# A DLRM tower on one core: when the second quad's rows are gathered and turned, and where the last sum over d stands

## The chip, the cores and the metric

One NeuronCore of a Trainium2 chip runs the whole program. The metric is device time of one execution in microseconds (us), as the median of three runs. Engines are named as the profile names them: PE is TensorE, ACT is ScalarE, DVE is VectorE, POOL is GpSimd, SP is SyncE, which here only issues DMAs.

## The reference

```python
e = jnp.stack([tbl_0[ids[:, 0]], ..., tbl_38[ids[:, 38]]], axis=1)   # (512, 39, 16)
Xi = X0 = e
for W, b in Ws:                                                      # three layers, H = 128
    Wr = W.reshape(H, F0_, Fi)
    Xi = jnp.einsum('hjk,bjd,bkd->bhd', Wr, X0, Xi) + b[None, :, None]
    res.append(Xi.sum(axis=2))
z = jnp.concatenate(res, axis=1)                                     # (512, 384)
h = jnp.concatenate([z, dense_ctx], axis=1)
h = jnp.maximum(h @ W_top1 + b_top1, 0.0)
h = jnp.maximum(h @ W_top2 + b_top2, 0.0)
y = h @ W_top3
```

Everything is float32. B = 512 batch rows, F = 39 fields, D = 16.

## The kernel before

The batch is cut in 32 tiles of 8 rows (8 rows by 16 d are 128 columns); four tiles are a quad, and there are 8 quads. I write (ti, g) for group g of tile ti in a quad; T counts tiles from 0 to 31.

**Gathering a quad.** POOL fetches its rows with ten indirect DMAs, `gather(q, g)` (L495). They are then regrouped into `emb_room`: for the first two quads by copies on the engines (`regroup`, L347), later by DMAs of SP. POOL repeats them down `emb_room` (`repeat_rows`, L507 and L509, signal `emb_made`), PE turns them (`turn_rows`, L1059, signal `emb_turned`), and ACT copies the result to `x0` (`keep_x0`, L657, signal `x0_made`).

**Layer 0 of a quad.** When `x0_made` comes, SP issues 12 copies inside SBUF: four for `xa` (L367) and eight for the windows of `bz` (L390; two of them for chunk 1, six for chunks 2 to 5), then eight more for the last chunk. POOL multiplies chunk by chunk (`multiply(q, c)`, L526): chunk 0 waits for the four copies, chunk 1 for its two, chunk 2 for all six. PE sums the chunks into `ps_x1` (`layer0`, L1096), one chunk after a group of the tile that `SECOND_SUMMED_AFTER` names: chunk 0 after (1, 9), chunk 1 after (2, 1), chunk 2 after (2, 3), chunk 3 after (2, 5).

**Layer 1 of a tile.** PE makes ten groups (`layer1`, L1191 to L1193: three matmuls into one of five banks of `ps_y`, signal `y_made`). ACT scales seven of them into `prod` (L740), DVE the other three, groups 2, 5 and 8 (L962, L964). A group waits for the bank to be read by whoever had it five groups ago. DVE reduces `prod` in two steps: `reduce_early(T)` (L972), and `reduce_late(T)` (L980). In tiles 0, 3, 4 and 7 and from tile 8 on, POOL first adds two pairs (`add_groups(T, 0)` and `(T, 1)`, L531), and `reduce_early` waits for both. ACT scales group 0 of tile T + 1 only after `reduce_early(T)`. PE sums over d with `sum_d(T)` (L1215), ACT keeps it (`keep_g`, L749).

**What sets the order** is written by hand: each engine runs its own list strictly in order and waits on semaphores. For quad 1, POOL issues gathers 2 to 9 each behind a step of the head (the first quad's rows, x0, xa, products, sum); then `add_groups(0, 0)`, half of the regrouping, `repeat_rows(1)`, `add_groups(0, 1)`, the index of quad 2 and its first seven gathers, then `multiply(1, c)`. The other half of the regrouping is ACT's, after group 3 of tile 0. PE turns quad 1's rows after group 7 of tile 0, and ACT's `keep_x0(1)` follows at the same place.

**The end.** Layer 2 is folded into one matmul loop over the 39 fields (L1262 to L1264), whose weights come by DMA from DRAM; the known parts of the first dense layer (`known_mlp1`: L1203 for the dense features, L1209 for parts 0 and 1) are put in around it. The split of the dense features into high and low parts is ACT's (L782, L783) and DVE's (L1035, L1037) in tile 29.

Of the kernel before, what the change touches and what calls it, by code (L numbers as in the profile page):

```python
# [5 lines left out]
ALU = mybir.AluOpType  # L6
# [3 lines left out]
F32 = mybir.dt.float32  # L10
# [3 lines left out]
P = 128  # L14
# [5 lines left out]
TILES = B // TB  # L20
# [3 lines left out]
QUADS = TILES // QT  # L24
# [8 lines left out]
CHUNKS = STEP + 1  # L33
# [6 lines left out]
GATHERS = -(-F // FPG)  # L40
# [68 lines left out]
SECOND_REGROUPED_AFTER = 3  # L109
NEXT_TURNED_AFTER, NEXT_KEPT_AFTER = [(0, 7), (0, 1)], [(0, 7), (0, 3)]  # L110
# [68 lines left out]
def build(nc, dense_ctx, ids, bases, table, W_top1, b_top1, W_top2, b_top2, W_top3, W0, b0, W1, b1, W2, b2, out):  # L179
# [8 lines left out]
    with ExitStack() as ctx:  # L188
# [290 lines left out]
        def _(pool):  # L479
# [13 lines left out]
            def gather(q, g):  # L493
                n = gather_rows(g)
                pool.indirect_dma_start(  # L495
                    out=rows[0:n, q % 2, g, :], out_offset=None, in_=table,
                    in_offset=bass.IndirectOffsetOnAxis(ap=index[0:n, q % 2, g:g + 1], axis=0),
                ).then_inc(gathered[q % 2], 16)
# [47 lines left out]
            pool.wait_ge(regrouped_dve, 1)  # L546
            gather(1, 2)
            pool.wait_ge(emb_made, 1)
            gather(1, 3)
            pool.wait_ge(first_x0, 1)  # L550
            gather(1, 4)
            pool.wait_ge(first_xa, 1)
            gather(1, 5)
            pool.wait_ge(first_z, 2)
            gather(1, 6)
            pool.wait_ge(first_z, 4)
            gather(1, 7)
            pool.wait_ge(first_summed, 1)
            gather(1, 8)
            pool.wait_ge(first_x1_lo, 1)  # L560
            gather(1, 9)

            add_groups(0, 0)
            pool.wait_ge(pool_step, 1)
# [74 lines left out]
            for T in range(FREE_QUADS * QT, TILES):  # L639
                for part in range(2):  # L640
                    add_groups(T, part)
                    between(T // QT, T % QT, part)

        @block.scalar
        def _(act):
# [105 lines left out]
            for T in range(TILES):  # L751
# [3 lines left out]
                for g in ACT_GROUPS:  # L755
# [14 lines left out]
                    if (T, g) == (0, SECOND_REGROUPED_AFTER):  # L770
                        act.wait_ge(gathered[1], 16 * GATHERS)
                        for f in range(FPG // 2):
                            ins = regroup(nc.scalar.copy, 1, f)
                        ins.then_inc(regrouped_act, 1)
# [4 lines left out]
                    if (T, g) == (TILES - 3, 4):  # L779
                        act.wait_ge(late_mlp, 16 * 6)  # L780
                        act.wait_ge(z_used, CHUNKS * QUADS)
                        nc.scalar.copy(dense_stack[0:C, :], dense_t[:]).then_inc(dense_hi_made, 1)  # L782
                        nc.scalar.copy(dense_w_stack[0:C, :], wt1[0:C, K1 // P, :]).then_inc(dense_hi_made, 1)  # L783
# [28 lines left out]
        def _(dve):  # L812
# [174 lines left out]
            for T in range(TILES):  # L987
# [45 lines left out]
                if T == TILES - 3:  # L1033
                    dve.wait_ge(dense_hi_made, 2)
                    nc.vector.tensor_tensor(dense_low, dense_t[:], dense_stack[0:C, :].bitcast(F32),  # L1035
                                            ALU.subtract).then_inc(dense_lo_made, 1)
                    nc.vector.tensor_tensor(dense_w_low, wt1[0:C, K1 // P, :], dense_w_stack[0:C, :].bitcast(F32),  # L1037
                                            ALU.subtract).then_inc(dense_lo_made, 1)
# [14 lines left out]
        def _(pe):  # L1053
# [195 lines left out]
            pe.wait_ge(act_step, ACT_STEPS * (TILES - 1) + ACT_GROUPS.index(YBANKS + 1) + 1)  # L1249
            for m in range(2):  # L1250
                known_mlp1(m, (3, 0))
            sum_d(TILES - 1)
            for part in (3, 0):
                for m in range(2, MC1):
                    known_mlp1(m, (part,))
            pe.wait_ge(g_kept, TILES)
# [8 lines left out]
            for m in range(MC1):  # L1265
                known_mlp1(m, (1,))
# [50 lines left out]
```

## Time and profile before

| | us |
|---|---|
| median of 3 runs (range) | 677.99 (677.51 to 680.46) |
| the profiled execution, its own time | 682.74 |
| span of the profiled execution | 680.5 |
| busy: PE, ACT, DVE, POOL | 654.7, 572.2, 518.0, 460.1 |
| PE's granted clock over the span | 0.992 |

A timeline row gives the start, the busy time, the engine, the line, what is written and read, the count, and in brackets the idle time before it and what ended it. Times are from the start of the span. The profiled execution took 2.2 us outside its span, and 4.75 us more than the median.

### The profile page before, as it was taken

How to read it: one execution, taken by the hardware profiler on the slowest of the kernel's cores; microseconds unless marked ns; L12 is line 12 of the kernel's file. 1: busy time of each engine (PE TensorE's matmuls, PEld its weight loads, DVE VectorE, ACT ScalarE, POOL GpSimd, SP SyncE). 2: the span in 40 equal slices, each digit the busy share in tenths (PEclk: the TensorE clock that was granted, in tenths of full speed). 3: DMA queues.
4: the chain of work that ended last, by engine and by line, in shares of the span. 5: the costliest groups of instructions: out<-in, count | busy, mean ns of one | idle time of the engine just before them, and what ended most of it. 6: DMA issues, size and time to landing. Idle time of an engine off the chain costs nothing. (4 is left out here: it accounts for less than half of the span.)

```text
span 680.5 us, 10678 instructions
## 1 busy us (share of the span) xinstructions
PE 654.7 (96%) x2692; PEld 480.2 (71%) x2692; DVE 518.0 (76%) x1017; ACT 572.2 (84%) x2013; POOL 460.1 (68%) x453
## 2 busy tenths in 40 slices
PE   3699999999999999999999999999999999999998
PEld 3566776677777777777777677767777777776673
DVE  5458796787878879697878778777868787888880
ACT  2467897889898989899999889888988899899772
POOL 6468779877787878787887888777878656333000
PEclk9789999999999999999999999999999999999999
DMA  7203143323342516142331313131313221204400
GB/s 212 57 14 101 8 104 68 74 54 89 92 118 35 175 15 189 15 137 44 110 70 37 83 20 99 16 103 16 97 12 95 24 71 41 89 1 134 176 0 0
DMA packets 111121, 49.22 MB, mean 72 GB/s; under 512 B 82907, under 2 KB 94903, under 8 KB 111060
## 3 DMA queue, kind: packets, MB, share of 16 engines
q1 hardware_dynamic: 104830, 45.94, 25.6%
q0 software_dynamic: 5376, 1.45, 2.2%
q10 hardware_dynamic: 854, 1.16, 0.7%
q8 instruction: 21, 0.34, 0.2%
q14 instruction: 40, 0.33, 0.2%
HBM read 13.81 MB, written 5.24 MB: 28 GB/s over the span
## 5 line engine op out<-in xcount | busy, mean ns | idle before, releaser
L740 ACT ACTIVATE prod<-ps_y,xt 128x128 f32<-128x128 f32 x1792 | 492.8, 428 | 63.4 <-PE ps_y L1193 57.4
L1191 PE MATMUL ps_y<-w_hi,x_hi 128*128 128x512 f32 (+1 forms) x640 | 304.0, 475 | 7.6 <-DVE x_lo L928 3.3
L1193 PE MATMUL ps_y<-w_hi,x_lo 128*128 128x512 f32 (+1 forms) x640 | 249.2, 389 | 0.0
L1192 PE MATMUL ps_y<-w_lo,x_hi 128*128 128x512 f32 (+1 forms) x640 | 249.2, 389 | 0.0
L531 POOL TENSOR_TENSOR prod<-prod 128x512 f32<-128x512 f32 x120 | 155.1, 1292 | 90.7 <-ACT prod L740 85.6
L964 DVE SCALAR_TENSOR_TENSOR prod<-ps_y,xt,prod 128x128 f32<-128x128 f32 x576 | 163.5, 342 | 38.0 <-PE ps_y L1193 37.6
L495 POOL DMA_INDIRECT rows<-in_table,index x160 | 153.9, 962 | 47.0 <-issue 32.4
L1191 PEld LDWEIGHTS ps_y<-w_hi,x_hi 128*128 128x128 f32 x640 | 120.3, 188 | 63.7 <-issue 21.3
L972 DVE TENSOR_REDUCE prod<-prod 128x128 f32<-128x1536 f32 (+1 forms) x64 | 116.3, 1818 | 51.8 <-ACT prod L740 42.7
L1192 PEld LDWEIGHTS ps_y<-w_lo,x_hi 128*128 128x128 f32 x640 | 120.9, 189 | 43.4 <-issue 20.9
L1193 PEld LDWEIGHTS ps_y<-w_hi,x_lo 128*128 128x128 f32 x640 | 120.5, 188 | 26.0
L526 POOL TENSOR_TENSOR room<-room 128x512 f32<-128x512 f32 (+2 forms) x90 | 115.8, 1294 | 2.9 <-DMA room<-room 2.7
L980 DVE TENSOR_REDUCE x<-prod 128x128 f32<-128x1536 f32 x64 | 111.8, 1747 | 5.8 <-issue 2.5
L1096 PE MATMUL ps_x<-room,w0t 117*128 117x512 f32 (+5 forms) x186 | 95.9, 596 | 0.8 <-POOL room L526 0.7
L1215 PE MATMUL ps_g<-bd,x 128*128 128x320 f32 x128 | 45.5, 437 | 1.2 <-DVE x L980 1.1
L962 DVE TENSOR_SCALAR prod<-ps_y,xt 128x128 f32<-128x128 f32 x128 | 38.4, 341 | 3.9 <-PE ps_y L1193 3.9
L1096 PEld LDWEIGHTS ps_x<-room,w0t 117*128 117x128 f32 (+5 forms) x186 | 34.1, 189 | 9.0 <-POOL room L526 2.2
L749 ACT COPY g_all<-ps_g 128x320 f32<-128x320 f32 x64 | 31.4, 491 | 3.3 <-PE ps_g L1215 3.3
L1215 PEld LDWEIGHTS ps_g<-bd,x 128*128 128x128 f32 x128 | 22.9, 188 | 9.6 <-DVE x L980 5.1
L797 ACT CAST g_hi<-g_all 128x512 fp32r<-128x512 f32 x39 | 23.9, 621 | 3.3 <-PE ps_y L1264 0.4
L872 DVE TENSOR_TENSOR bd<-ps_tr,mask 128x1248 f32<-128x1248 f32 x16 | 23.1, 1444 | 0.0
L507 POOL COPY emb_room<-emb_room 128x312 f32<-128x312 f32 x15 | 6.6, 443 | 24.1 <-DMA emb_room<-rows 22.1
(149 smaller groups left out, 378.8 us busy)
## 6 DMA issues: line engine op xcount, KB each, us to landing
room<-room SPq DMA_DIRECT2D x75, 234.0 KB
room<-room SPq DMA_DIRECT2D x45, 78.0 KB
emb_room<-rows SPq DMA_DIRECT2D x168, 5.0 KB
rows<-in_table,index POOLq DMA_INDIRECT x160
w_hi_dram<-g_all SPq DMA_DIRECT2D x5, 512.0 KB
w_lo_dram<-g_all SPq DMA_DIRECT2D x5, 512.0 KB
g_all<-in_L_rec_W SPq DMA_DIRECT2D x9, 256.0 KB
g_all<-in_L_rec_W SPq DMA_DIRECT2D x4, 512.0 KB, 3.8
```

The costliest lines, as they stand in the source:

```text
L495: pool.indirect_dma_start(out=rows[0:n, q % 2, g, :], out_offset=None, in_=table, in_offset=bass.IndirectOffsetOnAxis(ap=index[0:n, q % 2, ...
L526: nc.gpsimd.tensor_tensor(bz[0:r, c, :], window, left if c == LAST else xa[0:r, :], ALU.mult).then_inc(z_made, 1)
L531: nc.gpsimd.tensor_tensor(prod[:, SLOT[a]:SLOT[a] + 2], prod[:, SLOT[a]:SLOT[a] + 2], prod[:, SLOT[b]:SLOT[b] + 2], ALU.add).then_inc(pool ...
L740: ins = nc.scalar.activation(prod[:, SLOT[k] + m // 2, :, m % 2], ps_y[:, g % YBANKS, m * H:(m + 1) * H], ACT.Copy, scale=xt[:, q % 2, ti, ...
L964: ins = nc.vector.scalar_tensor_tensor(out=a, in0=y, scalar=x, in1=a, op0=ALU.mult, op1=ALU.add)
L972: nc.vector.tensor_reduce(prod[:, BIASED, :, 0], prod[:, EARLY if adds(T) else EARLY_FIRST].rearrange("p n h l -> p h n l"), AX_XY, ALU.ad ...
L980: nc.vector.tensor_reduce(x2[:, T % 2, :], prod[:, LATE[T % 2]].rearrange("p n h l -> p h n l"), AX_XY, ALU.add).then_inc(reduced, 1)
L1096: nc.tensor.matmul(ps_x1[:], w, z, start=c == 0, stop=c == summed(q)[-1]).then_inc(z_used, 1)
L1191: nc.tensor.matmul(y, hi, w1_hi[:, cols], start=True, stop=False)
L1192: nc.tensor.matmul(y, hi, w1_lo[:, cols], start=False, stop=False)
L1193: nc.tensor.matmul(y, lo, w1_hi[:, cols], start=False, stop=True).then_inc(y_made, 1)
L1215: nc.tensor.matmul(ps_g[:, 0:(F + 1) * TB], x2[:, T % 2, :], bd[:, T // QT % 2, T % QT].rearrange("p j b -> p (j b)"), start=True, stop=Tr ...
```

## The change

The second quad's gathers 2, 3 and 4 now wait for `first_x0`, `first_z` and `first_x1_lo`; gathers 5, 6 and 7 wait for the 1st, 3rd and 5th group of layer 1; then comes `add_groups(0, 0)`, and gathers 8 and 9 wait for the 6th and 7th group. ACT's half of the regrouping moves from behind group 3 of tile 0 to behind group 9; PE's turn of the rows and ACT's `keep_x0(1)` move from behind (0, 7) to behind (1, 1). The split of the dense features goes from ACT and DVE in tile 29 to POOL in tiles 29 and 30. At the end, the third bank's known parts and one of the fourth's stand before `sum_d(31)`, and part 1 of banks 0 and 1 before the loop over the fields.

```diff
-SECOND_REGROUPED_AFTER = 3
-NEXT_TURNED_AFTER, NEXT_KEPT_AFTER = [(0, 7), (0, 1)], [(0, 7), (0, 3)]
+SECOND_REGROUPED_AFTER = (0, 9)
+NEXT_TURNED_AFTER, NEXT_KEPT_AFTER = [(1, 1), (0, 1)], [(1, 1), (0, 3)]
...
             gather(1, 1)
-            pool.wait_ge(regrouped_dve, 1)
+            pool.wait_ge(first_x0, 1)
             gather(1, 2)
-            pool.wait_ge(emb_made, 1)
+            pool.wait_ge(first_z, 2)
             gather(1, 3)
-            pool.wait_ge(first_x0, 1)
+            pool.wait_ge(first_x1_lo, 1)
             gather(1, 4)
-            pool.wait_ge(first_xa, 1)
-            gather(1, 5)
-            pool.wait_ge(first_z, 2)
-            gather(1, 6)
-            pool.wait_ge(first_z, 4)
-            gather(1, 7)
-            pool.wait_ge(first_summed, 1)
-            gather(1, 8)
-            pool.wait_ge(first_x1_lo, 1)
-            gather(1, 9)
+            for g in range(5, 8):
+                pool.wait_ge(y_made, 2 * g - 9)
+                gather(1, g)
 
             add_groups(0, 0)
+            for g in range(8, GATHERS):
+                pool.wait_ge(y_made, g - 2)
+                gather(1, g)
             pool.wait_ge(pool_step, 1)
...
+                if T == TILES - 3:
+                    pool.wait_ge(late_mlp, 16 * 6)
+                    pool.wait_ge(z_used, CHUNKS * QUADS)
+                    nc.gpsimd.tensor_copy(dense_stack[0:C, :], dense_t[:]).then_inc(dense_hi_made, 1)
+                    nc.gpsimd.tensor_copy(dense_w_stack[0:C, :], wt1[0:C, K1 // P, :]).then_inc(dense_hi_made, 1)
+                if T == TILES - 2:
+                    pool.wait_ge(dense_hi_made, 2)
+                    nc.gpsimd.tensor_tensor(dense_low, dense_t[:], dense_stack[0:C, :].bitcast(F32),
+                                            ALU.subtract).then_inc(dense_lo_made, 1)
+                    nc.gpsimd.tensor_tensor(dense_w_low, wt1[0:C, K1 // P, :], dense_w_stack[0:C, :].bitcast(F32),
+                                            ALU.subtract).then_inc(dense_lo_made, 1)
...
-                    if (T, g) == (0, SECOND_REGROUPED_AFTER):
+                    if (T, g) == SECOND_REGROUPED_AFTER:
...
-            for m in range(2):
-                known_mlp1(m, (3, 0))
-            sum_d(TILES - 1)
-            for part in (3, 0):
-                for m in range(2, MC1):
-                    known_mlp1(m, (part,))
-            pe.wait_ge(g_kept, TILES)
+            for m in range(MC1 - 1):
+                known_mlp1(m, (3, 0))
+            known_mlp1(MC1 - 1, (3,))
+            sum_d(TILES - 1)
+            known_mlp1(MC1 - 1, (0,))
+            pe.wait_ge(g_kept, TILES)
+
+            for m in range(2):
+                known_mlp1(m, (1,))
             for j in range(F):
...
-            for m in range(MC1):
+            for m in range(2, MC1):
                 known_mlp1(m, (1,))
```

The four instructions that POOL gains in tiles 29 and 30 are the ones that ACT and DVE lose there.

POOL before, from the second quad's gather 2 to the first copy of the regrouping; in brackets what a row waits for:

```order
L495 DMA rows<-in_table,index 128x16 [waits regrouped_dve]
L495 DMA rows<-in_table,index 128x16 [waits emb_made]
L495 DMA rows<-in_table,index 128x16 [waits first_x0]
L495 DMA rows<-in_table,index 128x16 [waits first_xa]
L495 DMA rows<-in_table,index 128x16 [waits first_z] x2
L495 DMA rows<-in_table,index 128x16 [waits first_summed]
L495 DMA rows<-in_table,index 96x16 [waits first_x1_lo]
L531 TENSOR_TENSOR prod<-prod 128x512 [waits act_step]
L347 COPY emb_room<-rows 32x10x4 [waits emb_turned,gathered_1,pool_step]
```

POOL now, the same stretch:

```order
L495 DMA rows<-in_table,index 128x16 [waits first_x0]
L495 DMA rows<-in_table,index 128x16 [waits first_z]
L495 DMA rows<-in_table,index 128x16 [waits first_x1_lo]
L495 DMA rows<-in_table,index 128x16 [waits y_made] x3
L531 TENSOR_TENSOR prod<-prod 128x512 [waits act_step]
L495 DMA rows<-in_table,index 128x16 [waits y_made]
L495 DMA rows<-in_table,index 96x16 [waits y_made]
L347 COPY emb_room<-rows 32x10x4 [waits emb_turned,gathered_1,pool_step]
```

Three gathers have moved behind groups of layer 1, and two more behind the first addition as well; what follows them on POOL is as before.

ACT before, from the copy of `xa`'s rest to the first groups of tile 1 (four `L740` rows are one group):

```order
L719 COPY room<-ps_g 128x384
L740 ACTIVATE prod<-ps_y,xt 128x128 x12
L347 COPY emb_room<-rows 32x10x4 x8
L740 ACTIVATE prod<-ps_y,xt 128x128 x12
L723 ACTIVATE x_hi<-ps_x,columns 128x384
L657 COPY room<-ps_tr 128x16x4x8
L740 ACTIVATE prod<-ps_y,xt 128x128 x24
```

ACT now (its lines have moved by 8):

```order
L727 COPY room<-ps_g 128x384
L748 ACTIVATE prod<-ps_y,xt 128x128 x24
L731 ACTIVATE x_hi<-ps_x,columns 128x384
L748 ACTIVATE prod<-ps_y,xt 128x128 x4
L347 COPY emb_room<-rows 32x10x4 x8
L748 ACTIVATE prod<-ps_y,xt 128x128 x8
L665 COPY room<-ps_tr 128x16x4x8
L748 ACTIVATE prod<-ps_y,xt 128x128 x12
```

The regrouping stands behind all seven groups of tile 0, and `keep_x0(1)` (L657, now L665) behind two groups of tile 1.

PE before, from the end of layer 1 to the loop over the fields:

```order
L1203 MATMUL ps_tr<-g_hi 128x512
L1209 MATMUL ps_tr<-r,emb_room 128x512
L1203 MATMUL ps_x<-g_hi 128x512
L1209 MATMUL ps_x<-r,emb_room 128x512
L1215 MATMUL ps_g<-bd,x 128x320
L1203 MATMUL ps_y<-g_hi 128x512 x2
L1209 MATMUL ps_y<-r,emb_room 128x512 x2
L1262 MATMUL ps_y<-g_hi,w_hi 128x512
```

PE now (its lines have moved by 1 to 3):

```order
L1206 MATMUL ps_x<-r,emb_room 128x512
L1200 MATMUL ps_y<-g_hi 128x512
L1206 MATMUL ps_y<-r,emb_room 128x512
L1200 MATMUL ps_y<-g_hi 128x512
L1212 MATMUL ps_g<-bd,x 128x320
L1206 MATMUL ps_y<-r,emb_room 128x512
L1206 MATMUL ps_tr<-g_all,emb_room 128x512
L1206 MATMUL ps_x<-g_all,emb_room 128x512
```

Three more matmuls stand ahead of the sum over d, and two from behind the loop now stand ahead of it.

## Rows read from the trace of the kernel before

**Rows 1.** The page: busy time, share and instructions of each engine.

```profile
PE 654.7 (96%) x2692; PEld 480.2 (71%) x2692; DVE 518.0 (76%) x1017; ACT 572.2 (84%) x2013; POOL 460.1 (68%) x453
```

**Rows 2.** Waits of PE: total us, times, longest us.

```profile
PE ps_y L1191 <- DVE x_lo L928: 3.3, 1, 3.3
PE ps_y L1191 <- DVE x_lo L879: 2.5, 3, 1.4
```

**Rows 3.** Timeline of POOL around tiles 0 to 2.

```profile
35.48 0.92 POOL L495 DMA_INDIRECT rows<-in_table,index  x1 [0.30 <-issue]
...
39.79 2.49 POOL L347 COPY emb_room<-rows 32x40 f32<-32x40 f32 x8
44.09 0.44 POOL L507 COPY emb_room<-emb_room 128x312 f32<-128x312 f32 x1 [1.82 <-ACT emb_room L347]
...
45.23 1.30 POOL L531 TENSOR_TENSOR prod<-prod 128x512 f32<-128x512 f32 x1 [0.53 <-ACT prod L740]
...
46.98 1.00 POOL L495 DMA_INDIRECT rows<-in_table,index  x1 [0.28 <-POOL index L489]
...
56.78 1.30 POOL L526 TENSOR_TENSOR room<-room 128x512 f32<-128x512 f32 x1
...
61.70 1.31 POOL L526 TENSOR_TENSOR room<-room 126x512 f32<-126x512 f32 x1
```

**Rows 4.** Timeline of ACT: before layer 1, and in tiles 0 and 1.

```profile
34.06 0.37 ACT L715 ACTIVATE x_hi<-ps_x,columns 128x128 fp32r<-128x128 f32 x1 [6.47 <-remote]
...
42.12 1.85 ACT L347 COPY emb_room<-rows 32x40 f32<-32x40 f32 x8
...
48.66 0.59 ACT L657 COPY room<-ps_tr 128x512 f32<-128x512 f32 x1
49.88 4.25 ACT L740 ACTIVATE prod<-ps_y,xt 128x128 f32<-128x128 f32 x16 [0.64 <-PE ps_y L1193]
```

**Rows 5.** Timeline of DVE: the early reduction of tile 0.

```profile
49.12 1.74 DVE L972 TENSOR_REDUCE prod<-prod 128x128 f32<-128x1536 f32 x1
```

**Rows 6.** Timeline of PE in tiles 0 to 2.

```profile
47.87 0.75 PE L1059 MATMUL ps_tr<-ident,emb_room 128*128 128x128 f32 x4
...
49.44 0.40 PE L1193 MATMUL ps_y<-w_hi,x_lo 128*128 128x512 f32 x1
...
58.23 1.10 PE L1096 MATMUL ps_x<-room,w0t 128*128 128x512 f32 x2 [0.44 <-POOL room L526]
...
63.07 1.12 PE L1096 MATMUL ps_x<-room,w0t 126*128 126x512 f32 x2
```

**Rows 7.** Timeline of SP's queue: the window copies of quad 1.

```profile
52.44 6.29 SPq L390 DMA_DIRECT2D room<-room  x8
```

**Rows 8.** DMA issues: count, KB each, median us to landing.

```profile
g_hi<-g_hi SPq DMA_DIRECT2D x4, 32.0 KB, 1.9
```

**Rows 9.** Windows: stretch, busy us of PE, PEld, DVE, ACT, POOL, PEclk, DMA share, GB/s.

```profile
34.00:36.00 2.00, 1.13 (x4) 0.97 (x5) 1.33 (x4) 0.93 (x3) 1.47 (x2) 0.91 0.21 63
36.00:38.00 2.00, 2.00 (x5) 0.58 (x4) 0.67 (x3) 1.92 (x8) 0.40 (x1) 0.50 0.09 12
38.00:40.00 2.00, 2.00 (x7) 1.18 (x6) 0.13 (x1) 0.37 (x2) 1.48 (x2) 0.74 0.02 4
```

**Rows 10.** Timelines of PE, ACT and DVE in tiles 29 to 31 and after.

```profile
609.82 0.60 ACT L782 CAST g_hi<-dense_t 16x512 fp32r<-16x512 f32 x1
...
614.44 0.67 DVE L1035 TENSOR_TENSOR g_hi<-dense_t,g_hi 16x512 fp32r<-16x512 f32 x1
...
614.58 0.50 PE L1191 MATMUL ps_y<-w_hi,x_hi 128*128 128x512 f32 x1 [0.33 <-DVE prod L964]
...
618.47 0.50 PE L1191 MATMUL ps_y<-w_hi,x_hi 128*128 128x512 f32 x1 [0.23 <-DVE prod L964]
...
632.05 0.81 PE L1215 MATMUL ps_g<-bd,x 128*128 128x320 f32 x2 [1.09 <-DVE x L980]
```

**Rows 11.** All gathers (L495): ns min/median/max, first and last start.

```profile
L495 POOL DMA_INDIRECT rows<-in_table,index x160: 918/946/1155, 3.6 to 526.7; - x160
```

More of the change, by code:

```diff
@@ L778, in _ @@
                         keep_x0(q + 2)
[L779 to L783, printed above, removed]
                     if g == 7 and T > 0:
@@ L1032, in _ @@
                                             w2_home(False, n), ALU.subtract).then_inc(w2_lo_made, 1)
[L1033 to L1038, printed above, removed]
                 if T == TILES - QT:
```

## The prediction

> **What bounds the kernel now.** I read the page's busy line first [rows 1]: PE is busy 96% of the span, and no other engine is over 84%. The second view is the list of PE's waits [rows 2]. Its longest once matmuls run is 3.3 us before the first group of layer 1; the waits for `x_lo` at the quads' borders come to 2.5 us in three. From there on PE simply works through its list. So two things matter: an idle time of PE that the change adds is not won back later, because 650 us of work stand in a row behind it; and a relief of ACT, DVE or POOL brings only what PE waits for them.
>
> The third view is the timelines around tiles 0 to 2. They show that quad 1's layer 0 comes just in time. PE's chunk 0 waits 0.44 us for POOL at 58.23 [rows 6]. POOL's product of chunk 2 runs from 61.70 to 63.01 [rows 3], and PE takes it at 63.07 [rows 6]. So whatever delays POOL's chunk 2 by more than nothing delays PE as much, and everything after it.
>
> **The move of gathers, regrouping, turn and x0.** I follow what chunk 2 hangs on. Before, ACT regroups at 42.12, in a time when it would wait for PE, POOL repeats the rows from 44.09 to 44.70 (the addition at 45.23 has 0.53 us of idle time ahead of it), the addition ends at 46.53, and `keep_x0(1)` ends at 48.66 + 0.59 = 49.25 [rows 3, 4]. Now the same steps stand in this line, each waiting for the one before:
> - Group 9 of tile 0 is ready on PE at 49.84 (49.44 + 0.40) [rows 6]. The turn no longer stands ahead of it, which is 0.5 us: 49.3.
> - ACT scales it: 16 scalings took 4.25 us, so four take 1.1 [rows 4]: 50.4.
> - ACT regroups, 1.85 us [rows 4]: 52.3. It waits for all gathers. Gather 9 follows the seventh group, now at about 46.2. Its landing time is no row; before, POOL's regrouping at 39.79 did not wait for the gather issued at 35.48 [rows 3], so it lands within 4.3 us, by 50.5, and I cost this wait at nothing.
> - POOL repeats the rows, 0.6 us, and only then makes `add_groups(0, 1)`, 1.30 us [rows 3]; with handoffs of 0.05 to 0.1: 54.35.
> - DVE's `reduce_early(0)` waits for that addition, 1.74 us [rows 5]: 56.2. Before, it started at 49.12, so it is some 5 us late.
> - ACT's group 0 of tile 1 waits for that reduction, then group 1: 2.1 to 2.2 us. Only behind them stands `keep_x0(1)`, 0.59 us: 59.05.
>
> So x0 is ready at 59.05 instead of 49.25, 9.8 us later. PE meanwhile stops at the turn from about 50.7 to 53.1 (for `emb_made`) and at (1, 3) from 54.35 to 57.0 (for DVE's group 8, which stands behind the reduction). These idle times lie inside the delay of chunk 2 and are not added to it.
>
> From x0 to chunk 2 there are two paths. **POOL's own list:** the addition ends at 54.35 instead of 46.53; seven gathers at 0.95 + 0.30 us follow the index (which starts them 0.45 us after the addition), up to 63.3; then chunk 0, a gather, chunk 1, a gather, 2.46 us a pair: chunk 2 could start at 68.2. Before, it was 61.70 [rows 3], so this path alone costs 6.5 us. **SP's copies:** before, the last window is issued at 52.44 + 6.29 = 58.73 [rows 7], 9.5 us after x0; now at 68.5. A landing takes 1.9 us for the nearest transfer with a figure, 32 KB inside SBUF [rows 8]: 70.4, the lower bound. The upper bound is that the windows landed just before 61.70, 12.45 us after x0: 71.5. So chunk 2 is 8.7 to 9.8 us late. The copies are large and landed while other copies ran, so I take a value in the middle, **+9.3 us**.
>
> **PE's clock.** With chunk 2 at 71.0, its product is there at 72.3; PE has done (2, 3) by about 69.15 and is idle for 3.2 us. The one idle time of that length in the trace is the 3.3 us before layer 1 [rows 2]. After it the granted clock is 0.91, 0.50 and 0.74 in three stretches of 2 us [rows 9], which is 0.18 + 1.0 + 0.52 = 1.7 us of lost clock; that is 3.4 us at 1.2 GHz in place of 2.4. I expect the same once after chunk 2: 1.7 us, of which a wait of 0.4 us for chunk 3 covers a part: **+1.3 us**, bounds 0 and 1.7. The idle times at 50 to 57 may also lower the clock, but PE's next work ends ahead of POOL's chunk 0 (64.7) either way, so that costs nothing.
> The Trainium skill (TensorE: Matmul & The Clock Gate, What's actually happening) says that the slow state is the default and that activity releases it. By it even the shorter stops could bring the slow clock; the fall in the windows' rows agrees that idleness does, and no row here shows a shorter one that did.
>
> **The dense split.** ACT loses 1.2 us (0.60 and its twin) and DVE 1.3 us (0.67 and its twin) in tile 29, where both delay the banks: PE waits 0.33 us at 614.58 and 0.23 us at 618.47 for DVE's group 8 [rows 10]. These go: **-0.55 us**. On POOL the casts and subtractions stand in its idle time. They come about a tile later than DVE's at 614.44 [rows 10], near 622; four small copies of SP at some 0.6 us and a landing of 1.9 us [rows 8] make 626.5. PE asks for them when layer 1 is done, which is two banks of known parts (about 3 us) and the wait of 1.09 ahead of the sum at 632.05: near 627.9. So I cost this at nothing, but over 1.4 us more of delay would be a wait. The weights of the last loop are issued behind them, up to 2.6 us later than now, and are first wanted about 3 us after that sum.
>
> **The last sum over d.** PE waits 1.09 us for DVE's last reduction, until 632.05 [rows 10]. Three more known matmuls (about 1.5 us) now stand ahead of it, so the wait is covered; the amount of PE's work is the same, so what is won is the idle time: **-1.1 us**. ACT's copy and the first high and low parts come about 0.3 us later, and PE has the two matmuls of part 1 to do in that time.
>
> **Sum.** 9.3 + 1.3 - 0.55 - 1.1 = +8.95 us. Against the profiled execution (682.74) that is 691.7; it stands 4.75 us above the median of 677.99. I put the difference on the median: **686.9 us**. Nothing in the head before layer 1 hangs on the gathers except POOL's own list, so I cost their removal there at nothing; bounds are in the second rival.
>
> **Rivals.**
> A. *POOL's list decides, not the windows.* If the copies land sooner, because fewer gathers run beside them, chunk 2 is 6.5 us late, and PE's idle time there is 0.4 us with no slow clock: 678.0 + 6.5 - 1.65 = 682.8 us. Against it: the issue of the copies alone takes 9.5 us after x0.
> B. *The head starts earlier.* ACT's first `x_hi` waits until 34.06 for something that the profile cannot name [rows 4], while the eight gathers run. If they cause it, layer 1 starts up to 3.3 us sooner and the 1.7 us of slow clock there go too: 686.9 - 5.0 = 681.9 us. Against it: PE's sum, for which ACT waits, shares nothing with POOL that a row shows.
> C. *Not slower.* The same mechanism as B, in the head, at its full price of 5.0 us and with the 1.65 us of the end. It decides once the chain behind x0 costs less than 6.65 us; its lower bound is the 6.5 us of POOL's list, without a slow clock: 677.99 + 6.5 - 6.65 = 677.8 us.
> D. *More is lost.* The clock falls before chunk 3 and after it, or the stacked dense features come late by 1 to 2 us: 690 us.
> E. *Gathers slow down beside DVE's work.* Every gather took 0.92 to 1.16 us, in the head and beside layer 1 alike [rows 11]. If each of the seven ahead of chunk 0 had to sit out one reduction of DVE, 1.74 us [rows 5], chunk 0 and all behind it would come 12 us later: 699 us.
> The Trainium skill (SBUF — State Buffer, A bandwidth-pool intuition that's wrong) says that such a DMA waits for its descriptors while DVE holds a shared port, about 620 ns against 3100 ns. The range of 160 gathers does not bear this out here.
>
> **How the numbers follow.** Chances: the forecast 0.66 (own range 685 to 689), A 0.13, B 0.08, C 0.04, D 0.07, E 0.01; 0.01 for a faster outcome that I have not named. The range goes from A to the lower part of D: 682.5 to 689.8. A measurement of this kernel tells 0.5% from no change, 3.4 us: faster means under 674.6, slower over 681.4. C is no change, with the low edge of A and B (0.04); slower is the rest.
>
> **What would show it.** In the profile after: ACT's regrouping near 50.5 and its `x0` copy near 58.5; DVE's first early reduction near 54.4; PE waiting for `emb_room` and for `prod` in tile 1, then two or three waits at L1096's place for POOL's `room`, the longest about 3 us, and a granted clock of 0.50 around 73 to 77; no wait at 614 and at the last sum over d. I am wrong if `x0` is copied before 55, if chunk 2 starts before 69, or if layer 1 starts before 34.

## The result, and the profile after

The changed kernel takes 685.08 us (median of 5; 682.98 to 686.73), the kernel before 678.05 (5 runs) beside it. The medians are 7.0 us apart. The ratio of the two kernels' runs is 1.0096, with a 95% interval of 1.0069 to 1.0123: **6.5 us slower** (4.7 to 8.3). The profiled execution took 686.73 us with a span of 684.2, so its span is 3.7 us longer than that of before, whose profiled execution (682.74) was 4.7 us above its kernel's median.

PE's list of waits in the changed kernel (total us, times, longest us), for [rows 2]:

```profile
PE ps_y L1188 <- DVE prod L967: 3.8, 7, 2.2
PE ps_tr L1056 <- DVE emb_room L911: 3.4, 1, 3.4
PE ps_x L1093 <- POOL room L526: 3.1, 3, 2.6
PE ps_tr L1056 <- POOL emb_room L509: 2.5, 2, 2.1
PE ps_y L1188 <- DVE x_lo L882: 1.3, 1, 1.3
```

From layer 1 on, three new waits of over 2 us stand there: for `prod`, for POOL's product `room`, and for the repeated rows `emb_room`. The 3.3 us before layer 1 are gone, but the head has a new stop of 3.4 us, at the turn of the first quad's rows (`emb_room L911`), where before waits 0.3 us.

The chain behind quad 1's rows, timelines of the changed kernel: ACT, then POOL, DVE, SP's queue (as in [rows 3 to 5, 7]):

```profile
32.59 0.37 ACT L723 ACTIVATE x_hi<-ps_x,columns 128x128 fp32r<-128x128 f32 x1 [4.63 <-PE ps_x L1156]
...
47.40 1.85 ACT L347 COPY emb_room<-rows 32x40 f32<-32x40 f32 x8
53.11 2.19 ACT L748 ACTIVATE prod<-ps_y,xt 128x128 f32<-128x128 f32 x8 [3.86 <-DVE prod L975]
55.12 0.64 ACT L665 COPY room<-ps_tr 128x512 f32<-128x512 f32 x1
```
```profile
49.38 0.44 POOL L507 COPY emb_room<-emb_room 128x312 f32<-128x312 f32 x1 [1.40 <-ACT emb_room L347]
...
49.95 1.27 POOL L531 TENSOR_TENSOR prod<-prod 128x512 f32<-128x512 f32 x1
...
60.49 1.31 POOL L526 TENSOR_TENSOR room<-room 128x512 f32<-128x512 f32 x1
...
68.12 1.26 POOL L526 TENSOR_TENSOR room<-room 126x512 f32<-126x512 f32 x1 [2.71 <-DMA room<-room]
```
```profile
51.32 1.75 DVE L975 TENSOR_REDUCE prod<-prod 128x128 f32<-128x1536 f32 x1 [5.11 <-POOL prod L531]
```
```profile
55.78 3.13 SPq L367 DMA_DIRECT2D room<-room  x4
58.95 6.29 SPq L390 DMA_DIRECT2D room<-room  x8
```

The rows form one chain. ACT regroups; POOL repeats the rows (it was idle for 1.40 us, waiting for ACT) and then adds; DVE reduces (idle for 5.11 us, waiting for POOL); ACT scales two groups (idle for 3.86 us, waiting for DVE). Only then comes `x0`, which ends at 55.76. POOL's chunk 2 starts 12.36 us after that and waits 2.71 us **for a DMA**, so the window copies decide and not POOL's own list.

PE in tiles 0 to 2 of the changed kernel, for [rows 6]:

```profile
50.03 0.75 PE L1056 MATMUL ps_tr<-ident,emb_room 128*128 128x128 f32 x4 [2.12 <-POOL emb_room L509]
...
53.91 0.80 PE L1188 MATMUL ps_y<-w_hi,x_hi 128*128 128x512 f32 x1 [2.20 <-DVE prod L967]
...
61.95 1.10 PE L1093 MATMUL ps_x<-room,w0t 128*128 128x512 f32 x2 [0.23 <-POOL room L526]
...
69.44 1.12 PE L1093 MATMUL ps_x<-room,w0t 126*128 126x512 f32 x2 [2.59 <-POOL room L526]
```

Chunk 2 is at 69.44 where it was at 63.07 [rows 6]: 6.37 us late. Windows of the changed kernel (columns as in [rows 9]); the granted clock is the third number from the right:

```profile
36.00:38.00 2.00, 2.00 (x9) 1.47 (x9) 1.14 (x5) 0.63 (x3) 0.94 (x1) 1.00 0.06 16
...
48.00:50.00 2.00, 0.00 (x0) 0.00 (x0) 0.00 (x0) 1.19 (x6) 0.62 (x3) 1.00 0.00 0
50.00:52.00 2.00, 1.67 (x7) 0.97 (x7) 0.68 (x1) 0.00 (x0) 1.72 (x3) 0.77 0.00 0
52.00:54.00 2.00, 0.10 (x1) 0.10 (x1) 2.00 (x5) 0.89 (x4) 1.61 (x2) 0.50 0.03 4
54.00:56.00 2.00, 2.00 (x5) 1.61 (x6) 2.00 (x2) 2.00 (x8) 1.47 (x2) 0.50 0.09 7
...
68.00:70.00 2.00, 0.56 (x2) 0.32 (x3) 0.19 (x1) 0.09 (x1) 1.73 (x2) 1.00 0.13 31
70.00:72.00 2.00, 2.00 (x9) 1.25 (x8) 0.00 (x0) 0.63 (x3) 1.98 (x3) 1.00 0.13 25
```

PE's clock stays whole at the start of layer 1, where before it was 0.50. It stands at 1.2 GHz from about 51.2 to 57.6 instead. PE had been idle for 2.12 us before 50.03 and had worked again for some 1.2 us when the clock fell; its second stop, of 2.20 us, came only after that. The clock does **not** fall after the 2.59 us ahead of chunk 2.

The end, PE's sums over d of tiles 28 to 31 (before: tile 31 at 632.05 after 1.09 us of waiting [rows 10]):

```profile
614.67 0.70 PE L1212 MATMUL ps_g<-bd,x 128*128 128x320 f32 x2
622.58 0.70 PE L1212 MATMUL ps_g<-bd,x 128*128 128x320 f32 x2
630.08 0.70 PE L1212 MATMUL ps_g<-bd,x 128*128 128x320 f32 x2
637.50 0.81 PE L1212 MATMUL ps_g<-bd,x 128*128 128x320 f32 x2
```

No wait stands ahead of the last one.

### The profile page after: what moved, and what is told of

Its sections match the earlier page's. It is cut to its first block and busy times, and to the rows that moved or that the text cites. A ratio compares the mean times of both kernels' runs of the same rounds, so it can differ in the third digit from the quotient of the medians.

```text
span 684.2 us, 10678 instructions
## 1 busy us (share of the span) xinstructions
PE 657.3 (96%) x2692; PEld 482.6 (71%) x2692; DVE 517.4 (76%) x1015; ACT 571.6 (84%) x2011; POOL 464.8 (68%) x457
## 5 line engine op out<-in xcount | busy, mean ns | idle before, releaser
L495 POOL DMA_INDIRECT rows<-in_table,index x160 | 155.0, 969 | 52.7 <-issue 31.8
```

What stands on the lines that cost most here:

```text
L495: pool.indirect_dma_start(out=rows[0:n, q % 2, g, :], out_offset=None, in_=table, in_offset=bass.IndirectOffsetOnAxis(ap=index[0:n, q % 2, ...
```

## The experiments

In the table, before_again to e_keep ran on one chip, which I call the faster one, and e_list, e_sem, e_all and e_best on another, the slower one. The kernel before takes 668.8 and 669.0 us on the first and 678.7 us on the second; in the first comparison it took 678.05. A ratio is always against the kernel before beside it, and the microseconds are that ratio times before's median. Differences of medians deviate from them by up to 0.8 us in most rows, by 1.1 in e_keep and by 2.1 in e_list. The changed kernel itself was not run beside the last four. To compare traces I cut each span in four pieces: the start of ACT's first `x_hi`; from there to PE's chunk 2 of quad 1; from there to the sum over d of tile 28; and from there to the first matmul of the last part of the dense layer (L1269 before). All are read from the timelines.

| kernel | ratio (interval) | us against before | x_hi | to chunk 2 | to sum 28 | to the end's matmul |
|---|---|---|---|---|---|---|
| before | | | 34.06 | 29.01 | 546.45 | 56.48 |
| changed | 1.0096 (1.0069 to 1.0123) | +6.5 | 32.59 | 36.85 | 545.23 | 55.06 |
| before_again | 1.0005 (0.9991 to 1.0019) | +0.3 | 26.39 | 27.35 | 543.97 | 56.00 |
| after_again | 1.0127 (1.0106 to 1.0148) | +8.5 | 26.87 | 36.78 | 543.37 | 54.58 |
| e_turn | 1.0142 (1.0120 to 1.0165) | +9.5 | 26.26 | 36.70 | 543.95 | 55.97 |
| e_both | 1.0161 (1.0130 to 1.0191) | +10.8 | 25.30 | 36.96 | 543.12 | 56.00 |
| e_gath | 1.0039 (1.0023 to 1.0055) | +2.6 | 25.82 | 29.50 | 543.43 | 55.99 |
| e_end | 0.9991 (0.9973 to 1.0009) | -0.6 | 27.65 | 27.36 | 542.72 | 55.04 |
| e_tail | 0.9983 (0.9971 to 0.9996) | -1.1 | 25.48 | 27.48 | 543.67 | 55.50 |
| e_keep | 1.0079 (1.0060 to 1.0097) | +5.3 | 27.55 | 34.43 | 543.08 | 54.57 |
| e_list | 1.0089 (1.0060 to 1.0118) | +6.0 | 31.38 | 33.29 | 552.25 | 54.56 |
| e_sem | 1.0008 (0.9983 to 1.0034) | +0.5 | 30.98 | 34.41 | 544.69 | 54.58 |
| e_all | 1.0062 (1.0039 to 1.0085) | +4.2 | 29.71 | 33.50 | 548.57 | 54.58 |
| e_best | 0.9947 (0.9926 to 0.9968) | -3.6 | 34.27 | 28.88 | 544.09 | 54.58 |

### The turn alone, and with the gathers

The question was whether the earlier head of the changed kernel (rival B) belongs to the gathers. e_turn:

```diff
-SECOND_REGROUPED_AFTER = 3
-NEXT_TURNED_AFTER, NEXT_KEPT_AFTER = [(0, 7), (0, 1)], [(0, 7), (0, 3)]
+SECOND_REGROUPED_AFTER = (0, 9)
+NEXT_TURNED_AFTER, NEXT_KEPT_AFTER = [(1, 1), (0, 1)], [(1, 1), (0, 3)]
```

> The kernel before with ACT's regrouping behind (0, 9) and PE's turn and keep_x0(1) behind (1, 1); the gathers and the end are those of before. Theory G (the earlier head of the changed kernel comes from the gathers that left it): the head is that of before, the first x_hi of layer 1 starts near 34.0, PE runs at half clock at 36 to 38, x0 of quad 1 ends near 59, chunk 2 on PE starts near 72.5 instead of 63.07, and the time is about 9 us over before, 687 us. Theory V (the two profiled heads differed by chance, the gathers do nothing to them): the time is that of the changed kernel plus its 1.65 us at the end, 686.7 us, and the head's place in the trace may be either. Both theories give nearly one time here; it is the kernel with both moves that tells them apart.

e_both has in addition the change's edit of the gathers:

> The kernel before with the gathers moved and the regrouping, the turn and keep_x0(1) moved, that is the changed kernel without anything of its end. Theory G: the head is as in the changed kernel (first x_hi near 32.6, no half clock at 34 to 40), chunk 2 on PE near 69.4, and the time is 2.5 to 3.5 us under that of the kernel with the turn moved alone: 683.5 to 684.5 us if that is 687, and the end is then worth little. Theory V: the same time as the kernel with the turn alone, 686.7 us, and the end's edits are worth the 1.65 us that I gave them.

Measured: +9.5 us (8.0 to 11.0) and +10.8 us (8.7 to 12.8). The gathers gave nothing back here: on this chip theory V holds and rival B doesn't. Its head had no long wait to give back, as before_again shows below. The turn alone has the whole loss. POOL's chunk 2 in e_turn, then in e_both:

```profile
61.64 1.27 POOL L526 TENSOR_TENSOR room<-room 126x512 f32<-126x512 f32 x1 [1.57 <-DMA room<-room]
```
```profile
60.94 1.26 POOL L526 TENSOR_TENSOR room<-room 126x512 f32<-126x512 f32 x1 [2.84 <-DMA room<-room]
```

`x0` ends at 49.42 and 48.48 there, so chunk 2 starts 12.2 and 12.5 us after it, and in both it waits for the copies. On PE chunk 2 stands 36.70 and 36.96 us after the first `x_hi`, where before_again has 27.35 (below): **+9.4 and +9.6 us**.

### The gathers alone

```diff
+            pool.wait_ge(first_x0, 1)
             gather(1, 2)
+            pool.wait_ge(first_z, 2)
             gather(1, 3)
             pool.wait_ge(first_x1_lo, 1)
-            gather(1, 9)
+            for g in range(4, GATHERS):
+                gather(1, g)
```

> The kernel before with only the gathers moved: gathers 2, 3 and 4 behind first_x0, first_z and first_x1_lo as in the changed kernel, 5 to 9 straight behind 4; regrouping and turn stand where they were. Gather 9 is issued near 40.5 (33.4 + six times 1.2), lands by 44, so ACT's regrouping at 42.1 may wait some 2 us, and the turn with it. Theory G: layer 1 starts 1.5 us earlier and without half clock, which gives back up to 3.3 us; with some 1 us lost at the turn the time is 675 to 676.5 us. Theory V: no gain from the head, 678 to 680 us.

Measured +2.6 us (1.5 to 3.7), outside of what theory G expects (1.5 to 3 us faster) while theory V's 0 to +2 overlaps with the interval. ACT's regrouping in this kernel:

```profile
35.47 1.86 ACT L347 COPY emb_room<-rows 32x40 f32<-32x40 f32 x8 [2.98 <-DMA rows<-in_table,index]
```

It waits 2.98 us for the gathers, and chunk 2 is 2.15 us late (29.50 against 27.35). So even this small delay of quad 1's rows is paid in full, and nothing comes back in the head.

### Before and the changed kernel once more

> The kernel before, unchanged, for a second trace of it beside the runs of this call. Theory V (the head's delays of some microseconds belong to single executions, not to the gathers): PE's sum of the head comes 8 us after ACT's first regrouping, as with the turn moved alone, ACT names PE for its wait and not something remote, there is no half clock at the start of layer 1, and chunk 2 on PE starts 27.3 us after the first x_hi. Theory G (eight gathers in the head delay it): the long wait and the half clock of the first trace are there again, and the distance is 29.0 us. The time is that of the kernel before, ratio 1.000.

> The changed kernel, unchanged, beside the parts. Sum of the parts as measured: turn and gathers +10.3 us, the end -0.1 us by its median or -0.9 us by its trace: 9.4 to 10.2 us over before (ratio 1.0141 to 1.0152). If the 7.0 us of its first comparison hold here too (1.0105), the parts don't add up and something in the whole gives 3 us back. Chunk 2 on PE 36.9 us after the first x_hi, as in its first trace.

ACT's first `x_hi` in before_again:

```profile
26.39 0.37 ACT L715 ACTIVATE x_hi<-ps_x,columns 128x128 fp32r<-128x128 f32 x1 [3.16 <-PE ps_x L1159]
```

PE's chunk 2 in the same trace:

```profile
53.74 1.13 PE L1096 MATMUL ps_x<-room,w0t 126*128 126x512 f32 x2
```

The wait of 6.47 us for something remote in [rows 4] is 3.16 us for PE here, with the same gathers; there is no half clock after it. Chunk 2 follows 27.35 us after it. The first trace of before has 29.01, and the difference of 1.7 us is what [rows 9] lose to the clock. The changed kernel costs 8.5 us (7.1 to 9.9) on this chip, which overlaps with its first comparison; the 9.4 to 10.2 that I expected lie at the upper end of the interval or over it. Its span is 7.9 us longer (676.1 against 668.2): +0.5 at `x_hi`, +9.4 up to chunk 2, -0.6 in the long stretch, -1.4 at the end.

### The link through the reduction

One number of the changed kernel, so that `keep_x0(1)` stands right behind the regrouping:

```diff
-NEXT_TURNED_AFTER, NEXT_KEPT_AFTER = [(1, 1), (0, 1)], [(1, 1), (0, 3)]
+NEXT_TURNED_AFTER, NEXT_KEPT_AFTER = [(1, 1), (0, 1)], [(0, 9), (0, 3)]
```

> The changed kernel with one number changed: ACT's keep_x0(1) stands right behind the regrouping (after group 9 of tile 0) instead of behind the first two groups of tile 1, which wait for DVE's reduction, which waits for POOL's addition. Theory chain: x0 is ready 4.2 us earlier (18.9 us after the first x_hi instead of 23.1). The windows then land 31.3 us after x_hi, POOL's own list reaches chunk 2 32.8 us after it, so POOL's list decides, PE starts chunk 2 34.1 us after x_hi instead of 36.9, and the time is 2.7 us under the changed kernel. Rival: something other than x0's place in ACT's list holds the windows (the copies' landing beside the gathers): chunk 2 does not move and the time is the same.

Measured +5.3 us over before, 3.2 under after_again; chunk 2 34.43 us after `x_hi`, where 34.1 was expected. ACT and POOL in e_keep:

```profile
45.78 0.59 ACT L665 COPY room<-ps_tr 128x512 f32<-128x512 f32 x1 [1.57 <-PE ps_tr L1056]
```
```profile
55.69 1.31 POOL L526 TENSOR_TENSOR room<-room 128x512 f32<-128x512 f32 x1
58.17 1.30 POOL L526 TENSOR_TENSOR room<-room 127x512 f32<-127x512 f32 x1
60.64 1.29 POOL L526 TENSOR_TENSOR room<-room 126x512 f32<-126x512 f32 x1
```

`x0` waits for PE's turn alone and is done 18.82 us after `x_hi` instead of 23.2. Chunk 2 shows no wait for a DMA any more, though `x0` ended 14.3 us ahead of it: now POOL's list is the bound, as in rival A. This shows that the detour over addition, reduction and two groups held `x0`.

### The end

e_tail changes PE's order only; e_end adds the dense split as the change has it.

```diff
-            for m in range(2):
+            for m in range(MC1 - 1):
                 known_mlp1(m, (3, 0))
+            known_mlp1(MC1 - 1, (3,))
             sum_d(TILES - 1)
-            for part in (3, 0):
-                for m in range(2, MC1):
-                    known_mlp1(m, (part,))
+            known_mlp1(MC1 - 1, (0,))
             pe.wait_ge(g_kept, TILES)
+            for m in range(2):
+                known_mlp1(m, (1,))
...
-            for m in range(MC1):
+            for m in range(2, MC1):
                 known_mlp1(m, (1,))
```

> The kernel before with only PE's order at the end changed (three more known matmuls ahead of the last sum over d, part 1 of banks 0 and 1 ahead of the loop); the dense split stays on ACT and DVE. Prediction's step: -1.1 us. From the trace with the whole end changed: -0.43 us, of which the covered wait gives 1.05 and slower switching between the known matmuls and a slower loop over the fields (0.700 us a field instead of 0.687) take the rest. If the loop's pace belongs to the order of the matmuls it is 0.700 here; if it belongs to the dense split and its late DMAs it is 0.687 and the gain is 0.9.

> The kernel before with only the end changed: the split of the dense features on POOL, three more known matmuls ahead of the last sum over d, part 1 of two banks ahead of the loop. The prediction's sum gives -1.65 us: 676.35 us. Its head is that of before: theory G expects ACT's wait of 6.5 us and the first x_hi near 34.0 with half clock at 36 to 38 in this trace too, theory V expects that it may as well look like that of the changed kernel. From the changed kernel's trace (the delay goes from 5.15 us in tile 29 to 3.7 us at the end of the loop) the end is worth 1.0 to 1.5 us.

Measured -1.1 us (-1.9 to -0.3) for e_tail and -0.6 us (-1.8 to +0.6) for e_end. Taken alone, the second is no more than "no change". The traces are sharper. From the sum of tile 28 on, before_again, e_turn, e_both and e_gath need 56.0 us, and after_again and e_keep 54.6: 1.4 us less. e_tail and e_end ran their loop over the fields at another pace, 0.700 us a field instead of 0.687 (37 fields in 25.90 against 25.41 us), 0.5 us in all. At equal pace e_tail is at 55.0 and e_end at 54.6. So the order of the known matmuls is worth **1.0 us** and the dense split **0.4 us**. The pace belongs to neither edit, since before and changed ran at 0.700 in their first traces, and before_again and after_again at 0.687; what sets it stays open.

### The window copies

e_sem is the changed kernel with a semaphore of its own for chunk 2's two windows:

```diff
-                    cut_window(q, c, cut[q % 2])
+                    cut_window(q, c, (second_cut if c == 2 else cut)[q % 2])
...
                 if c == 2:
-                    wait(pool, cut[q % 2], 16 * WINDOWS * ((q + 1) // 2))
+                    wait(pool, second_cut[q % 2], 16 * len(window_parts(2)) * ((q + 1) // 2))
+                if c == 3:
+                    wait(pool, cut[q % 2], 16 * (WINDOWS - len(window_parts(2))) * ((q + 1) // 2))
```

> The changed kernel, only that chunk 2's two window copies have a semaphore of their own, and chunk 3 waits for the other four; no copy moves. Theory issue (the 12.4 us between x0 and chunk 2 are SP's issue of twelve copies, 9.5 us, and one landing of 2.9 us): chunk 2's second window is issued 6.4 us after x0 and lands at 9.3, so the windows no longer decide, POOL's list does, and PE starts chunk 2 at 34.3 us after x_hi instead of 36.8; the time is 2.5 us under the changed kernel (ratio 1.009). Rival landing (the copies share the rings and all land late together, 12 us after x0): chunk 2 moves by less than 1 us.

POOL in e_sem, chunks 2 and 3, with `x0` done at 54.18:

```profile
64.01 1.32 POOL L529 TENSOR_TENSOR room<-room 126x512 f32<-126x512 f32 x1
66.45 3.77 POOL L529 TENSOR_TENSOR room<-room 125x512 f32<-125x512 f32 x3
```

Chunk 2 starts 9.8 us after `x0`, with no wait for a DMA; its windows had landed by then, and chunk 3, which waits for the rest, starts 12.3 us after `x0` without a wait too. So the 12.2 to 12.5 us of the traces in which chunk 2 waits for the copies are SP's issue and the landing behind the last of twelve copies, as theory issue has it, and 34.41 us after `x_hi` is what was expected (34.3). The time is +0.5 us (-1.2 to +2.3) against before; I had expected +6. The changed kernel cost 6.5 and 8.5 us elsewhere, and about 2.4 us of that difference is chunk 2. The rest I can't assign: the changed kernel did not run beside this one, this kernel's runs lie between 674.24 and 683.26 us (and one at 684.58), and on this chip a share of before's time is a delay in the head (see the last section) which the changed head doesn't have. I take the trace's 2.4 us, and leave the rest open.

e_list is e_keep with three of quad 2's gathers ahead of chunk 0 and seven between the chunks; e_all is e_list with e_sem's edit.

```diff
-GATHERED_AT = {2: [0, 8, 9, 11, 13, 15, 17], 3: [0, 0, 0, 0, 38, 40, 42, 44, 46, 48],
+GATHERED_AT = {2: [0, 8, 9], 3: [0, 0, 0, 0, 38, 40, 42, 44, 46, 48],
```

> The kernel of the last call with keep_x0(1) behind the regrouping, and with three instead of seven of quad 2's gathers ahead of POOL's chunk 0; the other seven stand between the chunks. There POOL's list had become the bound (chunk 0 at 28.1 us after the first x_hi, no wait for a copy). Theory: the list is 5 us shorter ahead of chunk 2, so the windows decide again: they landed 12.2 to 12.5 us after the end of x0 in every trace, x0 ends 18.8 us after x_hi, so POOL's chunk 2 starts 31.2 and PE's 32.5 us after x_hi (34.4 without this edit), and the time falls by 1.9 us, to some 3.4 us over before (ratio 1.005). Rival (the four gathers beside the copies slow their landing): chunk 2 stays at 34, the time too.

> The three edits together on the changed kernel: keep_x0(1) behind the regrouping, three gathers ahead of chunk 0, own semaphore for chunk 2's windows. x0 ends 18.8 us after x_hi, chunk 2's windows land 9.3 us later, at 28.1, and PE could start it at 29.5 to 30 (before: 27.4). If nothing else is late in this stretch the time is 1 us over before, from +2.3 us at chunk 2 and -1.4 us at the end: ratio 1.001 to 1.002. If another wait appears (chunk 3 for the other windows, at 31.2 us on POOL and 32.5 on PE, where before it was 29.8), it costs up to 0.5 us more than that, since chunk 3 has the same 2.6 us to give. A ratio over 1.006 would say that the late turn costs by another way than chunk 2.

Measured +6.0 us (4.1 to 8.0) and +4.2 us (2.6 to 5.8): both expectations missed (+3.4, and +0.7 to +1.4), in two ways. For e_all I had written that a ratio over 1.006 would say that the late turn costs by another way than chunk 2; it is 1.0062. PE in e_list, where the turn, group (1, 3), chunk 0 and chunk 2 stand, and then quad 2's turn:

```profile
48.84 0.75 PE L1056 MATMUL ps_tr<-ident,emb_room 128*128 128x128 f32 x4 [2.12 <-POOL emb_room L509]
...
52.70 0.80 PE L1188 MATMUL ps_y<-w_hi,x_hi 128*128 128x512 f32 x1 [1.84 <-DVE prod L967]
...
60.17 1.02 PE L1093 MATMUL ps_x<-room,w0t 128*128 128x512 f32 x2
...
64.67 1.02 PE L1093 MATMUL ps_x<-room,w0t 126*128 126x512 f32 x2
...
88.86 1.13 PE L1056 MATMUL ps_tr<-ident,emb_room 128*128 128x128 f32 x4 [6.05 <-POOL emb_room L509]
```

First, PE waits for no chunk any more and is still 5.9 us late at chunk 2 (33.29 against 27.35). POOL's product of chunk 2 was ready at 63.97. It is PE that comes late: 2.12 and 1.84 us of waiting in tile 1, and some 2 us lost to half clock (0.50 in three stretches at 50 to 56). In the changed kernel the same losses lie hidden under the wait for the windows. Second, the later gathers make quad 2's rows late: its turn waits 6.05 us (3.37 in e_all). Half clock follows there too, 0.50, 0.50 and 0.54 in the stretches from 88 to 94, in which PE was busy for 5.1 us; that loses about 2.5 us more (1.7 in e_all). Together these are 8.5 of the 8.9 us by which the long stretch exceeds after_again's, and in e_all 5.1 of 5.2. This edit moved the wait to the next quad: the other way is the gathers of quad 2, not the late turn.

e_all also confirms what e_sem showed. With `x0` done at 48.54, chunk 2 starts 9.4 us after it without a wait for a DMA, and chunk 3 waits for the other four windows until 12.45 us after it:

```profile
60.99 1.28 POOL L529 TENSOR_TENSOR room<-room 125x512 f32<-125x512 f32 x1 [0.58 <-DMA room<-room]
```

### A version against before

e_best is the kernel before with the change's end and e_sem's semaphore; gathers, regrouping and turn stay.

> The kernel before with the changed end (both parts) and the semaphore of its own for chunk 2's windows: gathers, regrouping and turn as before. In every trace of the old head PE waits only 0.3 us for chunk 0 and 0.2 us for chunk 2, so the semaphore is worth at most 0.2 us here; the end is worth 1.4 us by the traces at equal pace of the loop. 667.5 us where before is 668.9, ratio 0.998. If the end's gain is real but smaller than 0.5 us, the ratio is 0.999 to 1.000, as the first run of the end's edits gave.

Measured -3.6 us (-5.0 to -2.2), **faster than before**, and by more than the expected 0.998, which lies outside the interval (0.9926 to 0.9968). It did not run beside the changed kernel, which is slower than before in both its comparisons. Its trace gives 1.9 us at the end (54.58 against 56.48; 1.4 at equal pace), and 2.4 us in the long stretch, which I don't credit to the edit: before_again has 543.97 there without any edit, and e_best 544.09, so it was the first trace of before that was long. That trace has the 2.5 us of waits for `x_lo` at the quads' borders of [rows 2]; before_again has none of them, e_best 1.2 us, and what brings them is not shown. Of the 3.6 us, 1.4 are accounted for.

## Why the prediction was right, and where not

I forecast 686.9 us, +8.95. Measured were 685.08 us, by the ratio +6.5 us (4.7 to 8.3), and +8.5 us (7.1 to 9.9) on the faster chip. The sign and the path were right. The size was near, partly by luck: it holds 1.3 us for a slow clock that did not come where I put it.

- **x0 late, and with it chunk 2: +9.3 us. Right.** e_turn and after_again give +9.4 us from the first `x_hi` to chunk 2, and `x0` is 9.5 us late in both (23.2 us after `x_hi` against 13.7 in before_again), where I had 9.8. The links came in the order that I wrote. `x0` was forecast 25.0 us after `x_hi` (59.05 less 34.06); it is 23.17 after it, and most of the 1.8 us is the half clock of [rows 9], which the changed kernel's trace doesn't have: before's own distance is 15.19 with it and 13.66 without. So in the pair of traces that I forecast, chunk 2 is only 6.4 us late, since the head took back 1.5 us and its clock 1.7. Two of my signs of being wrong came true by this: chunk 2 on POOL started at 68.12, before 69, and layer 1 before 34, with `x_hi` at 32.59. `x0` was copied at 55.12, hardly after the third limit of 55.
- **Windows against POOL's list. Right.** The 12.45 us that I had from one distance in before are 12.2 to 12.5 in e_turn, e_both, after_again and before_again. A landing behind the last issue took 2.9 us (65.24 to 68.12 in the changed kernel), near my upper bound. Rival A is what e_keep became, once `x0` was early enough.
- **Clock after chunk 2: +1.3 us. Wrong.** The clock is 1.00 at 66 to 72 behind a wait of 2.59 us, and in after_again behind one of 2.37. The step that failed is "I expect the same once after chunk 2". The half clock came in tile 1 instead, behind a wait of 2.1 us at the turn, in all eight traces with the late turn. In seven of them it fell before the second stop of tile 1 began (in e_turn at 43.6, before the turn itself), in e_keep 0.1 us after. The Trainium skill (TensorE: Matmul & The Clock Gate, What's actually happening) says that activity releases a slow default; by that both stops could bring it, and the trace agrees for the shorter stop alone. My step "that costs nothing" holds only as long as the windows are later: in e_list it was part of the price.
- **The dense split: -0.55. The size is nearly right, the waits only in part.** It is -0.4 us in the traces. Of the two waits that I counted, the one at 614.58 stayed (0.27 us at 619.68 in the changed kernel, where it was 0.33), so my "no wait at 614" failed; the other is gone, and the stretch from the sum of tile 29 to that of tile 30 took 7.50 us instead of 7.91. POOL's four instructions ran at 616.59 to 627.03 in the changed kernel, and nothing waited for them.
- **The last sum over d: -1.1. Right in kind.** The wait is covered, and 1.0 us is won at equal pace of the loop.
- **Rival B, the head: unlikely, and open where it matters.** The first pair of traces seemed to bear it out: `x_hi` 1.5 us earlier, no half clock. On the faster chip it is excluded. See below for the slower one.
- **Rival C** fell: its mechanism would need 5 us from the head, and the chain costs 9.4. **Rival D** did not occur in the changed kernel. **Rival E** fell: all gathers of the changed kernel took 918/947/1422 ns (lowest, median, highest), where [rows 11] have 918/946/1155, and POOL's seven gathers ahead of chunk 0 stand 1.25 us apart (once 1.56) while DVE reduces.

Without the clock's term my sum is 7.65 us, between the two measurements and near the 7.9 us by which the spans of before_again and after_again differ.

## What to carry to other kernels

Before a step is moved behind later work on one engine, write down what every engine's list puts between it and its consumer: here a copy moved by two groups waited for an addition, a reduction and two scalings of another tile, and every microsecond of it reached the bound engine, since the windows had no slack. When one wait covers others, taking it away shows them: of the 9.4 us, moving `x0` alone gave 2.4 back, and behind it stood POOL's list, then PE's own stops and its half clock. In this kernel a wait for the last of twelve copies was a wait for the issue of all of them, and a semaphore for the first user's part moved chunk 2 by 2.4 us in e_sem.

## What the runs showed that I had not expected

- **The head before layer 1 differs by chip.** With one program, the first `x_hi` starts at 34.06 and at 26.39, and its runs take 667.45 to 672.1 us on the faster chip and 675.3 to 681.07 on the slower one. Where before takes 678 us there are also stops in the head whose cause no row names. Two rows of ACT: from the first trace of before, and the first `x_hi` in e_best, which has the gathers of before:

```profile
17.86 0.58 ACT L688 COPY w0t<-ps_y 128x512 f32<-128x512 f32 x1 [3.68 <-remote]
```
```profile
34.27 0.37 ACT L730 ACTIVATE x_hi<-ps_x,columns 128x128 fp32r<-128x128 f32 x1 [6.62 <-remote]
```

  The second is the wait of [rows 4] again, with PE's 3.42 us and the half clock behind it. Where before takes 678 us it is there in both traces with the old gathers and in none of the four with the new ones (changed, e_list, e_sem, e_all), whose first `x_hi` starts at 29.71 to 32.59. Three of these four have another stop of PE instead, of 2.9 to 3.7 us at the turn of the first quad's rows, so the delay is in part moved and not gone. This would be theory G at work where the head is slow, and could be why the changed kernel lost 6.5 us there and 8.5 on the faster chip. The intervals overlap, and no kernel with the gathers alone ran there, so it stays open.
- **The loop over the fields has two paces**, 0.700 and 0.687 us a field, for the same instructions; 0.5 us over the loop.
- **An idle time of 2.1 us of PE was followed by half clock and one of 2.6 us was not**, 20 us later in the same execution. In these traces the length of a stop alone does not tell which one costs the clock.
